# Six-block decoder kernel: a sum and a choice moved within VectorE's pair, fill products in the first pair, one load awaited on its own

## What is computed

```
x = LN(x + attn0(x)); x = LN(x + xattn0(x, ctx)); x = LN(x + ffn0(x))
x = LN(x + diff_attn(x)); x = LN(x + latent_attn(ctx, x, mask)); x = LN(x + moe(x))
```

## Time and profile before

| what | us |
|---|---|
| three runs | 1658.73, 1660.99, 1661.41 |
| median | 1660.99 |
| the profiled execution: device time | 1658.21 |
| the profiled execution: span of the trace | 1656.5 |
| busy: TensorE / its weight loads | 1577.7 (95%) / 1327.1 (80%) |
| busy: VectorE / ScalarE / GpSimd | 1232.4 (74%) / 918.1 (55%) / 676.5 (41%) |
| mean granted TensorE clock | 0.991 |

### The profile page before, as it was taken

The page is one execution under the profiler, slowest core; times in us unless marked ns, Lnnn a source line. Parts: engine busy times, 40 slices in busy tenths (PEclk is TensorE's granted clock), DMA queues, the critical chain, the costliest instruction groups (busy, mean ns, idle before and its releaser), DMA issues. The chain is left out here.

```text
span 1656.5 us, 51937 instructions
## 1 busy us (share of the span) xinstructions
PE 1577.7 (95%) x18069; PEld 1327.1 (80%) x18069; DVE 1232.4 (74%) x3513; ACT 918.1 (55%) x2620; POOL 676.5 (41%) x1068
## 2 busy tenths in 40 slices
PE   7999999999999999999999999899999999999795
PEld 5887788787777777777777777799999999999664
DVE  6889888676777777677777776578888888888654
ACT  5777777643544444554445544566666666666241
POOL 3666655412333333333333333234444444444346
PEclk9999999999999999999999999999999999999897
DMA  3214221121220001111000000121212212122231
GB/s 106 65 48 120 71 57 56 45 60 51 51 54 26 25 25 30 27 29 28 25 25 25 25 26 27 40 59 45 62 47 56 60 43 62 48 56 58 71 113 40
DMA packets 157654, 82.30 MB, mean 50 GB/s; under 512 B 17641, under 2 KB 153115, under 8 KB 157568
## 3 DMA queue, kind: packets, MB, share of 16 engines
q1 hardware_dynamic: 154800, 77.68, 17.5%
q0 software_dynamic: 2048, 3.15, 0.6%
q10 hardware_dynamic: 720, 0.33, 0.1%
HBM read 61.03 MB, written 21.27 MB: 50 GB/s over the span
## 5 line engine op out<-in xcount | busy, mean ns | idle before, releaser
L1486 PE MATMUL bank<-diff_xT,diff_w_score 128*128 128x128 f32 x2048 | 256.4, 278 | 0.7 <-ACT diff_xT L1603 0.7
L1486 PEld LDWEIGHTS bank<-diff_xT,diff_w_score 128*128 128x128 f32 x2048 | 238.7, 192 | 22.4 <-issue 20.2
L1610 ACT ACTIVATE diff_keys<-bank 128x512 f32<-128x512 f32 x256 | 152.3, 595 | 161.7 <-PE bank L1486 161.7
L2085 ACT ACTIVATE lat_prob<-bank,lat_neg_max 128x128 f32<-128x128 f32 x512 | 180.6, 367 | 81.2 <-DVE lat_neg_max L2239 79.6
L1800 POOL TENSOR_TENSOR diff_prob<-diff_prob,diff_inv_sum 128x512 f32<-128x512 f32 x64 | 67.1, 1049 | 369.4 <-DVE diff_inv_sum L1703 369.4
L2301 POOL TENSOR_TENSOR lat_prob<-lat_prob,lat_inv_sum 128x512 f32<-128x512 f32 x128 | 133.4, 1042 | 131.5 <-DVE lat_inv_sum L2217 130.6
L2010 PE MATMUL bank<-lat_catT,lat_query 128*128 128x128 f32 x1024 | 139.3, 279 | 4.7 <-ACT lat_query L2096 4.7
L1978 PE MATMUL bank<-lat_catT,lat_w_score 128*128 128x128 f32 x1024 | 138.6, 279 | 3.8 <-issue 2.5
L1988 PE MATMUL bank<-lat_probT,lat_c_rep 32*128 32x256 f32 x2048 | 121.2, 384 | 14.9 <-DVE lat_z L2222 14.6
L1998 PE MATMUL bank<-lat_w_vo,lat_ctxT 128*128 128x128 f32 x1024 | 130.3, 275 | 1.1 <-ACT lat_ctxT L2108 1.1
L2010 PEld LDWEIGHTS bank<-lat_catT,lat_query 128*128 128x128 f32 x1024 | 125.3, 193 | 6.4 <-ACT lat_query L2096 5.1
(11 more groups left out here) (274 smaller groups left out, 3678.1 us busy)
## 6 DMA issues: line engine op xcount, KB each, us to landing
lat_c_rep<-cat SPq DMA_DIRECT2D x128, 128.0 KB
stage<-low_y SPq DMA_DIRECT2D x64, 64.0 KB, 1.6
diff_x_rep<-stage SPq DMA_DIRECT2D x128, 32.0 KB, 1.7
lat_c_t<-cat SPq DMA_DIRECT2D x32, 128.0 KB, 2.1
exp_w<-in_L_ffn_w_dram SPq DMA_DIRECT2D x16, 256.0 KB
expert_rows<-latw_zeros SPq DMA_DIRECT2D x4, 548.0 KB, 5.5
exp_rows<-expert_rows SPq DMA_DIRECT2D x8, 274.0 KB
low_x_t<-in_x_dram SPq DMA_DIRECT2D x32, 64.0 KB, 1.8
```

The source lines that it names most:

```text
L1486: last = nc.tensor.matmul(ring[(k + d) % 2][:, j * P:(j + 1) * P], w_score[:, H1 * (k // 2) + HS * d + 4 * (k % 2) + j, :], xT[:, :], star ...
L1610: nc.scalar.activation(keys[:, k // 2, 4 * (k % 2):4 * (k % 2) + 4, :].rearrange("p h t -> p (h t)"), ring[(k + d) % 2][:, :], ACT.Copy).t ...
L2085: last = nc.scalar.activation(prob[:, q, m, :], ps_s[q][:, m * T:(m + 1) * T], ACT.Exp, bias=neg_max[:, q, m:m + 1], accum_out=row_sum[:, ...
```

## The change

Four things. In the latent slots, VectorE's sum z moves from behind the transpose and the reciprocal of part 2 to the front of part 2; its statistics stay where they were. `choose_expert` moves from the end of part 1 to the end of part 2, except in slots 33 and 34. In slot 0, TensorE issues three products of constants after the first transposes and three after each of the four groups of queries. At the start, each group of loads has its bias rows on a semaphore of their own, which GpSimd alone awaits, in slot 2; TensorE transposes x before it waits for the copied weights, and transposes the cross weights after the values' products.

```diff
 class EarlyLoads:
-    def __init__(self, core, ctx, tag, parts):
+    def __init__(self, core, ctx, tag, parts, later=()):
         self.loaded, self.all, self.parts = core.sem(f"{tag}_loaded"), 16 * len(parts), []
+        self.later_loaded = core.sem(f"{tag}_later_loaded") if later else None
...
-    parts += [("bias_rows", [P, D], bcast_rows(bias), lambda t: t[:, :])]
-    return EarlyLoads(core, ctx, tag, parts)
+    return EarlyLoads(core, ctx, tag, parts, [("bias_rows", [P, D], bcast_rows(bias), lambda t: t[:, :])])
...
@@ LowHeads.tensor, slot
-            if isinstance(i, int) and i == -1:
-                cross_weights()
             if on(-1):
...
             if on(1):
                 w = int(cr(1))
+                if isinstance(i, int) and i == -1:
+                    pe.wait_ge(self.w_copied, 5)
                 wait(pe, self.xT_ready, i + 2)
...
                 last.then_inc(self.v_done, 1)
+            if isinstance(i, int) and i == -1:
+                cross_weights()
...
         pe.wait_ge(self.consts.ident_done, 1)
-        pe.wait_ge(self.w_copied, 5)
         self.slots(pe, slot, between)
@@ LowHeads.gpsimd
             if on(-2):
+                if isinstance(i, int) and i == 2:
+                    for loads in self.loads:
+                        pool.wait_ge(loads.later_loaded, 16)
...
-        for loads in self.loads:
-            pool.wait_ge(loads.loaded, loads.all)
         self.slots(pool, slot, between)
@@ latent stage, tensor: transpose_cat(i), and pair(i, par)
                 last.then_inc(ct_done, 1)
+                if isinstance(i, int) and i == 0:
+                    core.keep_busy(ps_c[3], 3)
...
                         queries(n, c, par)
+                        if isinstance(i, int) and i == 0:
+                            core.keep_busy(ps_c[3], 3)
@@ latent stage, vector: pair(i, par)
                     q = c % 2
+                    if c == 2 and live(i - 2):
+
+                        dve.wait_ge(res_loaded, 16 * (i - 1))
+                        dve.wait_ge(o_done, i - 1)
+                        nc.vector.tensor_tensor(z[:, :], x_res[:, :], ps_o, ALU.add).then_inc(z_done, 1)
                     if live(i) if c > 1 else live(i - 1):
...
                     if c == 2 and live(i - 2):
-
-                        dve.wait_ge(res_loaded, 16 * (i - 1))
-                        dve.wait_ge(o_done, i - 1)
-                        nc.vector.tensor_tensor(z[:, :], x_res[:, :], ps_o, ALU.add).then_inc(z_done, 1)
                         dve.wait_ge(z_done, i - 1)
                         nc.vector.bn_stats(stats[:, :], z[:, :]).then_inc(st_done, 1)
...
-                    if c == 1 and live(i - 3):
+                    if c == (1 if last(i, 1) or last(i, 2) else 2) and live(i - 3):
                         choose_expert(i, par)
```

More of the change, by code:

```diff
@@ L96 @@
 class EarlyLoads:
-    def __init__(self, core, ctx, tag, parts):
+    def __init__(self, core, ctx, tag, parts, later=()):
         self.loaded, self.all, self.parts = core.sem(f"{tag}_loaded"), 16 * len(parts), []
+        self.later_loaded = core.sem(f"{tag}_later_loaded") if later else None
         self.tile = {}
-        for name, shape, source, view in parts:
+        for n, (name, shape, source, view) in enumerate(parts + list(later)):
             if name not in self.tile:
                 self.tile[name] = core.sb(f"{tag}_{name}", shape, F32, ctx)
-            self.parts.append((view(self.tile[name]), source))
+            self.parts.append((view(self.tile[name]), source, self.loaded if n < len(parts) else self.later_loaded))
     def transfers(self):
-        return [(tile, source, self.loaded) for tile, source in self.parts]
+        return self.parts
     def start(self, eng, first=0, end=None):
```

## The result

The changed kernel took 1645.18 us (median of six runs, 1642.87 to 1651.83), the kernel before beside it 1660.78 us. The ratio is 0.9891, with a 95% interval from 0.9862 to 0.9920: faster by 1.1%. The forecast was 1653.2 us, in a range from 1645.5 to 1658.5 us. The direction was right, the size was not: the gain is twice what was forecast, and the time lies 0.3 us under the range. The profiled execution took 1644.60 us, with a span of 1642.7 us, 13.8 us less than before.

What follows compares the result with a forecast made beforehand. The prediction took a closed loop of contexts, VectorE's copies to z, and contexts as the latent stage's bound. Gains of 5.9 + 1.1 + 1.3 - 0.5 = 7.8 us gave 1653.2 us against the median of 1660.99 us, range 1645.5 to 1658.5 us.

Steps and rivals of the forecast that it cites:

- The closed loop: Latent stage: contexts, VectorE from its copies to z, then contexts again set the pace, 15.71 us a round.
- VectorE's new round: Latent loop after the change: eight steps from copies to copies summed to 15.52 us, above TensorE's 15.23 us, so VectorE binds.
- the unknown step: On VectorE, from `rstd` to the choice's first operation, not in the trace: taken as 0.33 us, between 0.1 and 0.61 us.
- my own bound: TensorE's own round in the latent loop: 15.71 - 0.48 = 15.23 us at the least.
- the first rival: TensorE becomes the bound: each of 28 rounds gives 0.48 us, 13.4 us, for 1645.7 us in all; chance 0.2.
- The 28 rounds: Latent loop: 0.19 us saved a round, 5.3 us, plus about 0.6 us once in the first rounds, together 5.9 us.
- The sign that I named for the first rival: In the latent loop, VectorE still waiting for the contexts before its copies would show TensorE as the bound.
- My sign of being wrong: Latent loop: the prediction is wrong if a round is over 15.7 us or under 15.3 us.
- What the choice's move is worth: Between part 1's maximum and z: the choice's 1.11 us taken out, besides 0.71 us of transpose and reciprocal.
- Slot 32: The choice stood in front of z there; z and what follows move up, 1.1 us gained.
- The first slot: First latent slot: constants' products keep TensorE's clock, 1.7 us, less 0.1 us at each of four groups: 1.3 us gained.
- The start: Later cross weights' transposes delay VectorE's second copies by 1.07 us and the scores of pair 1: 0.5 us lost.

Runs made afterwards that it cites:

- e1: The kernel before with only VectorE's sum z moved to the front of part 2, the choice left at the end of part 1: 1653.27 us, ratio 0.9939.
- e2: The kernel before with only the choice moved to the end of part 2 (except slots 33 and 34), z left in place: 1658.58 us, ratio 0.9984.
- e11: The changed kernel with the cross weights' transposes back in front of the keys' product, run again with more rounds: 1646.45 us, ratio 0.9884.
- e10: e1 plus a second statistics of z on VectorE in each slot, run once: rounds of 15.62 and 15.23 us.
- e4: The kernel before with the start's part alone (bias rows awaited apart, cross weights transposed after the values' products): 1661.88 us, ratio 0.9989.

## Why the prediction was wrong, point by point

- **The closed loop** of contexts, VectorE and z was right: with z first, TensorE's waits for z in the loop are gone but for one of 0.21 us (e1), and in the changed kernel all of them.
- **VectorE's new round is the step that failed**, and with it "so VectorE binds". The 15.52 us of my sum are 15.25 us in the trace: copies to maximum 8.98 instead of 9.05, maximum to reciprocal 2.26 as taken, to the statistics 0.09 for 0.06, to `rstd` 1.93 for 1.97, the unknown step to the choice 0.18 for 0.33, the choice 1.12 for 1.11, transpose and reciprocal to the copies 0.69 for 0.74 us. 0.15 of the 0.27 us are the step that no row showed. The round was then not above TensorE's, at 15.23 us by my own bound, but level with it, and the first rival, TensorE as the bound, was the case: 13.01 us for 13.4 us forecast under it. The 28 rounds give 13.0 us where I took 5.9. (They run from the third contexts to the thirty-first; from the fourth, as I wrote, it would be 27.) The 0.29 us between a sum of eight terms and the bound of 15.23 us decided it, and I put 0.58 on one side of it and 0.2 on the other. The sign that I named for the first rival, VectorE waiting for the contexts before its copies, is not there in the loop: the two rounds are only 0.03 us apart, VectorE's the longer one. My sign of being wrong, a round under 15.3 us, is there.
- **What the choice's move is worth** was read wrongly with it. I counted its 1.11 us as taken out of z's way, on top of the 0.71 us of transpose and reciprocal. z does start that much earlier, but the loop had use for 0.48 us only, and e1 shows that the 0.71 us are enough. By itself the late choice gives the loop nothing: e2 shows that its 1.11 us lay beside the exponentials. In my own list for the new order the reciprocal comes 2.26 us after the maximum, bound by these, and it does so in the old order too once the choice is gone.
- **Slot 32**: 1.11 us for 1.1 us forecast.
- **The first slot**: 1.6 us for 1.3 us in this pair of traces; no group of queries came out late. That the clock's fall is a matter of chance I had not said: all five traces without the products have the same idle times of TensorE just before the first scores, 1.06, 0.56 and 0.78 us, and the clock fell in four of them.
- **The start**: 0.5 us lost was forecast, about 0.7 us is the mean of the traces and 1.6 us was in this one, more than my upper end of 1.1 us. 0.87 us of it, at the scores of pair 1, is the mechanism named; the 0.73 us of low clock behind the long wait I had not counted. VectorE entered its slots 1.35 us later (14.66 us for 13.31 us), where I took 1.07 us: the keys' product started at 6.52 instead of 6.4 us and the stretch from it to the end of the values took 3.0 instead of 2.84 us, so that VectorE's second copies came at 10.62 instead of 10.35 us.
- **Not forecast at all**: 1.46 us lost in the middle and 1.23 us gained in the end, from low stretches of the clock that differ from one execution to the next (in the middle 3.4 us at half the clock, from 315.0 us on, in the changed kernel's trace and none in that of the kernel before; at the end 6.8 us against 10.2 us).

## What to carry to other kernels

Where the rounds of two engines lie within a few tenths of a microsecond of each other, the sum of a chain cannot say which will bind; give both cases their chance, and look for the one price that decides between them. A step is worth what lies in its place once it is gone: 1.1 us of work beside a wait of 2.3 us for another engine is free to leave where it is. When loads are awaited apart to start one engine sooner, ask first which engine's entry the pipeline hangs on; here TensorE's first product with the weights started 2.5 us earlier, and the scores of pair 2 came 0.7 us later in the mean.

## What the runs showed of the hardware

The granted clock of TensorE falls to half for short stretches at certain places of this kernel, and not in each execution. At the border behind the low heads, near 306 to 316 us, 12 of 14 traces show one, of 3.4 us in most, 13.7 us in e11 and 17.1 us in e10; the traces of the kernel before and of e4 show none. A single pair of traces therefore carries some 1.5 us of chance at each such place, as large as the first slot's part of this change or the start's. With products of constants in waits of 0.6 to 0.8 us the clock of the first latent slot stayed full in nine of nine traces, and without them in one of five.
